# Moving GpSimd's low half of a head group's output two tiles forward in a causal-attention loop

## What is computed

```
q, k, v = x @ Wq, x @ Wk, x @ Wv              # 16 heads of 32 columns
scores  = (q @ k.T) * tril(ones)              # masked by zeros, not by -inf
attn    = softmax(scores / sqrt(512))
out     = (attn @ v) @ Wo
```

## Time and profile before

| | |
|---|---|
| median of 3 runs | 1476.02 us (1475.46 to 1476.39) |
| profiled execution, its own time | 1477.08 us |
| span in the profile | 1475.4 us |
| TensorE busy | 1421.8 us, 96% |
| VectorE busy | 990.7 us, 67% |
| ScalarE busy | 713.2 us, 48% |
| GpSimd busy | 387.3 us, 26% |
| L784 `out_head` on GpSimd | 12 times, 611 ns each |
| L788 `out_tail` on GpSimd | 12 times, 1159 ns each |

### The profile page before, as it was taken

One profiled execution on the slowest core, in us unless ns is written; L12 is line 12 of the kernel. 1 busy time (PEld: TensorE's weight loads), 2 busy tenths in 40 slices (PEclk: granted clock), 3 DMA queues, 4 the chain that ended last, 5 costly groups with the idle time before them and its releaser, 6 DMA issues.

```text
span 1475.4 us, 26841 instructions
## 1 busy us (share of the span) xinstructions
PE 1421.8 (96%) x8896; PEld 719.6 (49%) x8896; DVE 990.7 (67%) x2125; ACT 713.2 (48%) x1648; POOL 387.3 (26%) x703
## 2 busy tenths in 40 slices
PE   6989998998999999999999999999999999999999
PEld 4465456556645654344444444444444444444444
DVE  7786688668658867886566666665655756665533
ACT  5795279339716945344354353353343443533532
POOL 0053225204374436521221212112112211212100
PEclk9999999999999999999999999999999999999999
DMA  7554522352465521000100001001001001000011
GB/s 249 135 167 125 162 80 81 100 159 84 123 179 152 187 77 46 17 28 21 33 14 19 17 17 33 17 17 35 17 17 32 17 17 33 17 17 1 0 58 57
DMA packets 77309, 98.01 MB, mean 66 GB/s; under 512 B 8048, under 2 KB 60784, under 8 KB 76784
## 3 DMA queue, kind: packets, MB, share of 16 engines
q1 hardware_dynamic: 77168, 96.23, 21.3%
HBM read 68.94 MB, written 27.26 MB: 65 GB/s over the span
## 4 chain that ended last, share of the span: by engine, by line
PE 84%; issue 5%; DVE 4%; ACT 3%; POOL 3%; DMA 0%; ACTq 0%; POOLq 0%; DVEq 0%; SPq 0%
PE bank L887 25%; PE bank L889 24%; PE bank L888 24%; PE bank L951 2%; PE bank L972 2%; ACT prob L1268 2%; POOL nmx L766 1%; PE bank L940 1%; PE bank L900 1%; PE bank L1012 1%; PE bank L1027 1%; POOL pk L759 1%; PE bank L981 1%; PE bank L1022 1%; DVE xt L1591 1%
## 5 line engine op out<-in xcount | busy, mean ns | idle before, releaser
L887 PE MATMUL bank<-xs,G 128*128 128x512 f16 x896 | 339.8, 379 | 2.0 <-DVE c L1736 0.9
L888 PE MATMUL bank<-xs,G 128*128 128x512 f16 x896 | 339.6, 379 | 0.0
L889 PE MATMUL bank<-xs,G 128*128 128x512 f16 x896 | 339.6, 379 | 0.0
L1354 ACT COPY c<-bank 128x512 f32<-128x512 f32 x192 | 111.4, 580 | 220.2 <-PE bank L889 215.4
L1736 DVE TENSOR_TENSOR c<-bank,c 128x512 f32<-128x512 f32 x128 | 88.1, 689 | 193.2 <-PE bank L889 193.2
L887 PE MATMUL bank<-Wd,hid 128*128 128x512 f16 x512 | 194.1, 379 | 2.8 <-DVE X L1790 2.8
L889 PE MATMUL bank<-Wd,hid 128*128 128x512 f16 x512 | 194.0, 379 | 0.0
L888 PE MATMUL bank<-Wd,hid 128*128 128x512 f16 x512 | 194.0, 379 | 0.0
L751 POOL TENSOR_TENSOR c<-c,m 128x512 f32<-128x512 f32 x64 | 82.4, 1287 | 388.7 <-ACT c L1354 388.7
L1790 DVE SCALAR_TENSOR_TENSOR X<-bank,col,X 128x512 f32<-128x512 f32 x128 | 95.3, 749 | 101.6 <-PE bank L889 101.4
L1606 DVE CUSTOM_DVE_ANT_0 bank<-bank,mask,col 128x128 f32<-128x128 f32 (+3 forms) x256 | 138.9, 547 | 22.7 <-issue 18.4
(11 more groups left out here) (193 smaller groups left out, 2401.1 us busy)
## 6 DMA issues: line engine op xcount, KB each, us to landing
stack<-qk_dram SPq DMA_DIRECT2D x128, 128.0 KB, 3.4
sc_in<-scale_t SPq DMA_DIRECT2D x30, 384.0 KB
qk_dram<-qk SPq DMA_DIRECT2D x32, 256.0 KB, 2.9
packed_t<-pk_t SPq DMA_DIRECT2D x32, 192.0 KB, 1.9
pk_in<-packed_t SPq DMA_DIRECT2D x30, 192.0 KB
X<-in_x_dram SPq DMA_DIRECT2D x4, 1024.0 KB, 5.9
pk_in<-L_ffn_gate_W_packed_dram SPq DMA_DIRECT2D x16, 256.0 KB, 2.8
pk_in<-n_L_ffn_up_W_packed_dram SPq DMA_DIRECT2D x16, 256.0 KB, 3.1
```

The costliest lines, as they stand in the source:

```text
L887: pe.matmul(o, lhs(0), rhs(0), start=first, stop=False, skip_group_check=onto)
L888: pe.matmul(o, lhs(0), rhs(1), start=False, stop=False, skip_group_check=onto)
L889: return pe.matmul(o, lhs(1), rhs(0), start=False, stop=stop, skip_group_check=onto)
L1354: nc.scalar.copy(dst[:], bank[BANK_Y if which == M5 else x][:]).then_inc(c_copied, 1)
```

## The change

`out_tail(n, r - 1)` is issued behind `shift` for j == 1, before `masked_values`, instead of behind `shift` and `convert` for j == 3. The instruction itself, its waits and the semaphore it raises are the same, and it still follows `out_head`. It is issued 12 times.

```diff
                         shift(n, u, j)
                         if j == 0 and i == 2 and r > 0:
                             out_head(n, r - 1)
+                        if j == 1 and i == 2 and r > 0:
+                            out_tail(n, r - 1)
                         if j == 1 and u > 0 and i > 0:
                             masked_values(n, u - 1)
                         if j > 0 and i > 1:
                             convert(n * (NB // B) + r, r, 3 * i + j - 7)
-                        if j == 3 and i == 2 and r > 0:
-                            out_tail(n, r - 1)
```

## The result

The changed kernel took 1481.70 us (median of 7, 1481.48 to 1483.38) against 1476.14 us (median of 7, 1475.46 to 1476.59): ratio 1.0040, interval 1.0031 to 1.0049. That is 5.6 us slower, where 4.6 was forecast, and the median forecast was 1480.6; in the profiled executions the spans are 1479.9 and 1475.4.

The account below looks back on a forecast made before the run. The chain ran through GpSimd's low half in attention, with ScalarE nearly as late; 6 x 0.52 + 2 x 0.76 + 4 x 0 gave 4.6 us slower, a median of 1480.6, range 1477.7 to 1483.0.

Parts of the forecast that it names:

- The place on the path: Attention: the chain near 92 us runs through GpSimd's low half for 0.49 us; extra GpSimd time there reappears whole in the period.
- GpSimd's new order: Low half ahead of v_zero and convert: head 2's negation 0.99 us late beside the norm tile, whose stretch is 0.19.
- ScalarE's 0.47 to spare: ScalarE from head 2's exponential to 95.14: of 4.30 us its own steps take 3.83, so 0.47 is waiting.
- VectorE: VectorE's 0.81 us wait for the low half goes; e_zero comes about 1.0 later, and its row maxima bind nothing.
- Head group 3: Four places in whose next unit the loop ends: taken as 0, between a gain of 0.25 and a loss of 1.0.
- head group 3's exit is unchanged: Sign that the forecast is right: the exit of head group 3 stays as it was, its term being 0.
- The bounds of -1.0 and +4.0: Limits given to head group 3's uncertain term, in us over its four places.
- The sum: 6 x 0.52 + 2 x 0.76 + 4 x 0 = 4.6 us slower: span 1480.0, median 1480.6.
- ScalarE catches up: Rival: ScalarE's steps between 90.84 and 95.14 hide waits, it regains 1.0 us; up to 4.3 faster, 1471.7; chance 8%.
- Half of it is regained: Rival: ScalarE only partly saturated or GpSimd idle, loss 0.3 or less a place; 2.0 slower, 1478.0; chance 13%.
- Nothing is regained: Rival: late e_zero holds VectorE's sums and row maxima, the 1.0 us passes whole at eight places; 10 slower, 1486; 6%.

Follow-up runs that it names:

- experiment 7: Kernel before, with the third convert of the 384-column unit made twice, ahead of the low half: 1481.91 us against 1476.41, ratio 1.0037.
- experiment 2: Changed kernel, with the low half behind masked_values and the convert, still ahead of head 2's negation: 1481.44 us against 1476.29 for the kernel before.
- experiment 6: Changed kernel, with VectorE's norm tiles moved to units 4, 5, 8 and 9: 1480.31 us against 1476.41 for the kernel before, ratio 1.0029.
- experiment 11: Changed kernel, with the three converts of the 384-column unit moved into the next unit: 1477.88 us against 1476.30 for the kernel before.
- experiment 1: Changed kernel, with the low half behind the third negation, ahead of the fourth: 1477.05 us against 1476.29 for the kernel before, ratio 1.0007.
- experiment 4: Kernel before, with VectorE making the low half ahead of its divide, GpSimd none: 1474.47 us against 1476.29, ratio 0.9987.
- experiment 5: Kernel before, with VectorE's norm tiles in units 4, 5, 8 and 9, none beside the 384-column tile: 1473.60 us against 1476.41.
- experiment 10: Kernel before, with three converts in the next unit, norm tiles in units 4, 5, 8, 9, and VectorE making the low half: 1471.59 us, ratio 0.9969.

## Why the prediction was right

**The place on the path.** Right: the chain ran through the low half, and in experiment 7 what was added to GpSimd's list ahead of it was paid whole. The prediction drew the same from two rows, a GpSimd stretch 0.31 longer beside the norm and a period 0.45 longer; those rows don't prove it, since 0.14 of the period is not in that stretch.

**GpSimd's new order.** Head 2's negation is 1.00 late (0.99 predicted). The stretch by the norm is 0.20 (1.36 against 1.16), 0.19 predicted from v_zero. The rule of the Trainium skill, page "SBUF — State Buffer", section "Who interferes with whom", has the second instruction wait for the whole of the first. The norm tile ends at 88.58 + 0.54 = 89.12 and the low half starts at 88.77, which makes 0.35. The row shows 0.20, so the sum goes by the row. The missing 0.15 is the same at every such meeting of the two engines (last section), so that one must take it off when pricing by the rule. That the norm tile is the cause is shown by experiments 2 and 6.

**ScalarE's 0.47 to spare.** It regained 0.50 (4.30 to 3.80). In experiments 2 and 11, and in the unit without the norm in experiment 6 and in the last sequence, the same stretch took 3.80 or 3.81 as well, whether it had been 4.30 or 4.07: so this is the floor that the prediction put at 3.83. The loss by the period is 0.55 in the first three sequences (0.52 predicted) and 0.80 in the last (0.76). Of the 0.55, 0.49 is the delay of the last exponential, counted from the high half, and 0.06 is that this exponential lasts longer (0.77 against 0.70), which the prediction did not have; why it does stays open.

**VectorE.** Its wait for the low half closed and e_zero was late next, without a price in groups 1 and 2: the negation that follows from it was done 0.67 us before ScalarE took it (94.14 and 94.81).

**Head group 3.** Here alone a place was off by more than a tenth: I took 0, and the sign "head group 3's exit is unchanged" did not come. From its high half to the next sequence's first, 101.88, 101.89 and 101.92 us stand against 101.70, 101.94 and 101.71: +0.18, -0.05 and +0.21. In the first sequence TensorE's turn comes 6.93 us behind the high half (126.45 - 119.52), where it came 6.75 (125.98 - 119.23). In the other three sequences it comes 6.94 or 6.95 behind, where it was 6.98, 6.75 and 6.74: in the second, VectorE's copy was late before the change already, so nothing was lost.

```profile
126.45 0.63 PE L951 MATMUL bank<-ident,prob 128*128 128x128 f32 x4 [0.16 <-DVE prob_t L1616]
```

In the row it waits 0.16 for VectorE's copy, which stands behind the late e_zero. The bounds of -1.0 and +4.0 held.

**The sum.** By periods: 3.34 at the six places with the norm, 1.59 at the two without and 0.34 in head group 3 make 5.3 us, against 4.6 predicted. From the last high half to the end it is 960.6 us against 960.5: the rest of the kernel only came later. The start of the profiled execution was 0.82 earlier than before, which leaves 4.5 between the two spans. That the span came out at 1479.9, as the 1480.0 of the forecast, is thus partly luck: the loss was 0.7 larger and the start 0.8 earlier. The 0.3 between 5.3 and the medians' 5.6 is within the spread of the runs.

**The rivals.** "ScalarE catches up" falls: at the places with the norm it regained 0.49 or 0.50 and no more, in the changed kernel and in every experiment where it was late (1, 2, 11). "Half of it is regained" falls by the periods: 0.55 and 0.80 are lost at a place, not 0.3 or less. "Nothing is regained" falls by the 0.50. What stays open is why ScalarE's exponentials of 384 columns have their fixed distances; no run changed its own list.

## What to carry to other kernels

An instruction on the critical chain isn't worth its duration but the wait of the next pacer: here 1.1 us on GpSimd held ScalarE up by 0.47, and by 0.24 where no norm tile stood beside it. To price a move inside an in-order list, add up the list between the old place and the new, and then subtract only the gaps that the engine behind really has. Look for work in the same list that nobody is waiting for at that point: moving three converts out of the way gained more than any place for the low half.

## What the runs showed of the hardware

**A clock drop in some executions.** In the profiled execution of the kernel before TensorE's granted clock was 0.57 in the stretch from 24 to 28 us, which is its lower level, 1.2 GHz, for most of it; in that of the changed kernel it was 1.00, 2.4 GHz. The view of a stretch gives its length, then busy time and count for PE, PEld, DVE, ACT and POOL, then the clock, the DMA share and GB/s. Before:

```profile
24.00:28.00 4.00, 4.00 (x13) 1.46 (x11) 3.74 (x6) 4.00 (x9) 0.00 (x0) 0.57 0.64 213
```

After:

```profile
24.00:28.00 4.00, 4.00 (x20) 1.44 (x19) 3.82 (x6) 4.00 (x9) 0.00 (x0) 1.00 0.59 195
```

Both kernels run the same program there, and 13 matmuls stand against 20. From 22 to 24 us, ahead of it, TensorE was busy for 0.75 us before and 0.67 after, at a granted clock of 1.00. This goes with the 0.82 us by which the attention of the changed kernel's profile is early, and the other profiles bear it out. Of all thirteen, six have a clock of 1.00 in this stretch, and the first high half starts at 87.6 to 88.0 us; the seven others have 0.57 to 0.74, and it starts at 88.4 to 89.0. Among the changed kernel's seven executions the three at 1482.5 to 1483.4 show a mean clock of 0.999 and the four at 1481.5 to 1481.7 one of 1.000, so it probably carries most of the spread too. What sets off the drop is not shown.

**How long GpSimd is held up beside VectorE.** In experiment 4 VectorE's low half has two inputs in SBUF. GpSimd's negation beside it takes 0.51 us instead of 0.19 and ends with it, as the timeline shows:

```profile
92.17 0.68 DVE L1647 TENSOR_TENSOR o_t<-o_sum,o_t 128x512 f16<-128x512 f32 x1
...
92.38 0.51 POOL L766 TENSOR_TENSOR nmx<-zero,mx 128x1 f32<-128x1 f32 x1 [0.48 <-DVE mx L1604]
...
92.94 0.29 DVE L1642 SCALAR_TENSOR_TENSOR o_sum<-bank,r_den 128x128 f32<-128x128 f32 x1
```

It ended at 92.89, the low half at 92.85. The Trainium skill, page "SBUF — State Buffer", section "Who interferes with whom", has a VectorE instruction with two SBUF inputs contend with a GpSimd instruction that reads SBUF, and the trace agrees. It cost nothing: ScalarE's next exponential started at 92.95, at its fixed distance of 1.02 from the one before.

The changed kernel's timeline has a negation beside a norm tile:

```profile
95.67 0.54 DVE L1579 TENSOR_SCALAR xn<-X,mv,rs 128x512 f32<-128x512 f32 x1
...
95.89 0.37 POOL L766 TENSOR_TENSOR nmx<-zero,mx 128x1 f32<-128x1 f32 x1 [0.28 <-DVE mx L1606]
```

When it starts, the norm tile has 0.32 us left, and it is stretched by 0.18. All the cases go by one difference:

| GpSimd instruction beside VectorE's | VectorE's time left | stretch | difference |
|---|---|---|---|
| negation, norm tile (95.89) | 0.32 | 0.18 | 0.14 |
| v_zero, norm tile (kernel before, 89.60) | 0.34 | 0.19 | 0.15 |
| low half, norm tile (88.77) | 0.35 | 0.20 | 0.15 |
| negation, low half (experiment 4, 92.38) | 0.47 | 0.32 | 0.15 |

The same holds wherever, in the traces of both kernels and of experiments 2, 4, 5 and 10, a GpSimd instruction starts 0.14 to 0.22 us behind one of these two VectorE instructions: with 0.32 to 0.47 us left, the stretch is what VectorE's record has left, less 0.13 to 0.15. So GpSimd was held up for the rest of the VectorE instruction, but for this constant; whether it belongs to the end of VectorE's record or to the start of GpSimd's isn't shown. A negation that starts only 0.05 to 0.07 us behind the norm tile isn't stretched at all (0.19 at 88.63, the norm tile at 88.58).
